# The scans of a hybrid block: VectorE's pieces in another order, squares and skip term in tiles of 64 columns

## What is computed

```python
x = x + conv_attention(group_norm(x))              # 1: softmax attention over 1024 pixels
t = to_tokens(x)                                   # 8 x 1024 tokens x 128
u = layer_norm(t)
xn = rmsnorm(u, norm_w)
z, xBC, dt = split(xn @ W_in.T)                    # 256 | 256+32+32 | 8
xBC = silu(causal_conv4(xBC) + conv_b)             # 4 taps along the tokens
xs, Bm, Cm = split(xBC)
dt = softplus(dt + dt_bias); dA = exp(-dt * exp(A_log))
state = state * dA + (dt * xs) B^T                 # a scan over the tokens, 8 heads of 32
y = state C + Dp * xs                              # Dp * xs is the skip term
y = rmsnorm(y * silu(z), gnorm_w)                  # needs the mean of (y * silu(z))^2
t = t + (u + y @ W_out.T)
t = t + mixture_of_8_experts(layer_norm(t))        # 3
```

## Time and profile before

| | us |
|---|---|
| three runs | 991.87, 996.23, 997.99 |
| median | 996.23 |
| profiled execution | 989.1 |
| its span, first to last instruction | 987.3 |
| busy in the span: TensorE / VectorE / ACT / GpSimd | 873.4 / 727.9 / 502.2 / 273.0 |
| granted TensorE clock, mean over the span | 0.95 |

### The profile page before, as it was taken

The page is one execution under the profiler, slowest core; times in us unless marked ns, Lnnn a source line. Parts: engine busy times, 40 slices in busy tenths (PEclk is TensorE's granted clock), DMA queues, the critical chain, the costliest instruction groups (busy, mean ns, idle before and its releaser), DMA issues.

```text
span 987.3 us, 18734 instructions
## 1 busy us (share of the span) xinstructions
PE 873.4 (88%) x7086; PEld 679.8 (69%) x7086; DVE 727.9 (74%) x1959; ACT 502.2 (51%) x740; POOL 273.0 (28%) x264
## 2 busy tenths in 40 slices
PE   3788999999989788898989797979789999999997
PEld 2556656655666666676767675757668888888887
DVE  2867678667867668576767777686868889888985
ACT  1525455545567564656565646464315544554453
POOL 0025111011000525242525252428513331233200
PEclk9979999999999789899979999989989999999999
DMA  5631011101101230303030303032000000000001
GB/s 146 187 136 22 1 22 22 22 1 22 23 1 30 45 75 1 74 2 74 2 74 2 74 1 75 2 74 66 2 1 1 22 23 22 2 22 22 23 1 43
DMA packets 30888, 36.07 MB, mean 37 GB/s; under 512 B 4560, under 2 KB 24912, under 8 KB 30800
## 3 DMA queue, kind: packets, MB, share of 16 engines
q1 hardware_dynamic: 29648, 30.68, 12.9%
q10 hardware_dynamic: 1152, 4.19, 1.2%
HBM read 21.50 MB, written 4.98 MB: 27 GB/s over the span
## 4 chain that ended last, share of the span: by engine, by line
PE 34%; DVE 18%; issue 4%; ACT 2%; POOL 2%; DVEq 0%; ACTq 0%; POOLq 0%
PE ps L1047 7%; DVE acc L1996 4%; PE ps L969 4%; PE ps L794 3%; PE ps L796 3%; PE ps L795 3%; DVE cacc L1712 2%; PE ps L960 2%; PE ps L948 2%; PE ps L953 1%; DVE dcy L1804 1%; PE ps L905 1%; PE ps L919 1%; PE ps L872 1%; PE ps L1088 1%
## 5 line engine op out<-in xcount | busy, mean ns | idle before, releaser
L1996 DVE SCALAR_TENSOR_TENSOR acc<-ps,comb,acc 128x128 f32<-128x128 f32 x512 | 139.8, 343 | 16.3 <-PE ps L1047 15.7
L1399 ACT ACTIVATE hid<-ps,b_f 128x512 f32<-128x512 f32 x128 | 87.2, 687 | 112.1 <-PE ps L796 112.0
L1047 PEld LDWEIGHTS ps<-w_f,hid 128*128 128x128 f32 x1024 | 130.6, 191 | 19.6 <-ACT hid L1399 8.1
L1047 PE MATMUL ps<-w_f,hid 128*128 128x128 f32 x1024 | 136.8, 277 | 5.2 <-ACT hid L1399 4.6
L1569 DVE TENSOR_REDUCE nmax<-ps 128x1 f32<-128x1024 f32 x64 | 78.1, 1220 | 29.8 <-PE ps L674 29.4
L1712 DVE SCALAR_TENSOR_TENSOR cacc<-ps,cw,cacc 128x1023 f32<-128x1023 f32 (+5 forms) x72 | 91.7, 1275 | 10.3 <-ACT cacc L1271 9.2
L570 POOL TENSOR_TENSOR srs<-sve,neg_half 128x1 f32<-128x1 f32 x64 | 53.8, 841 | 147.9 <-DVE gram L1821 147.8
L1187 ACT ACTIVATE probs<-ps,nmax 128x1024 f32<-128x1024 f32 x64 | 71.3, 1114 | 39.3 <-DVE nmax L1569 36.5
L969 PE MATMUL ps<-y_w 128*128 128x256 f32 x256 | 75.1, 420 | 12.8 <-DVE X L1831 12.2
L1340 ACT ACTIVATE dcy<-ps 128x1024 f32<-128x1024 f32 x64 | 65.1, 1017 | 40.8 <-PE ps L919 40.7
L1864 DVE TENSOR_TENSOR y_w<-ps,zs 128x256 f32<-128x256 f32 x64 | 27.0, 422 | 78.5 <-PE ps L960 76.0
(11 more groups left out here) (214 smaller groups left out, 1881.9 us busy)
## 6 DMA issues: line engine op xcount, KB each, us to landing
c_dec<-exp_dram SPq DMA_DIRECT2D x32, 256.0 KB, 5.1
xc<-in_x SPq DMA_DIRECT2D x8, 512.0 KB, 3.6
q_b<-q_a SPq DMA_DIRECT2D x16, 256.0 KB, 2.8
X<-in_x_tok ACTq DMA_DIRECT2D x8, 512.0 KB, 5.2
c_rep<-cacc SPq DMA_DIRECT2D x32, 128.0 KB, 5.9
out<-o_ch SPq DMA_DIRECT2D x8, 512.0 KB, 2.6
w_f<-in_w SPq DMA_DIRECT2D x2, 512.0 KB, 3.7
cst_f<-in_sel_rows SPq DMA_DIRECT2D x1, 512.0 KB, 4.3
```

The costliest lines, as they stand in the source:

```text
L1047: last = nc.tensor.matmul(ps[:, Y_BANKS[n], t * P:(t + 1) * P], hid[n % 2][:, t * P:(t + 1) * P], w2_f[:, e, :], start=True, stop=True)
L1399: nc.scalar.activation(hid[n % 2][:], ps[:, 4 + n % 2, :], ACT.Gelu, bias=b1_f[:, n // 2:n // 2 + 1]).then_inc(e_hidden_ready, 1)
L1996: done = nc.vector.scalar_tensor_tensor(acc[u][:, tt, :], ps[:, bank, t * P:(t + 1) * P], comb[u][:, tt, e:e + 1], acc[u][:, tt, :], ALU.m ...
```

## The change

Three things in the scans:

1. **Order.** `dve_parts` gets other slots: conv (0, 2) and (0, 3) join (0, 1) at slot 4 ahead of the gating; conv (1, 1) and (1, 2) go to slot 5; both halves of softplus to 5.5; conv (1, 3) to 6; `exponents` from 7.5 to 7, ahead of conv (2, 1); conv (2, 2) goes behind the end of the batch to -0.25 of the next and (2, 3) to its slot 0, behind `mixed` and `output`. TensorE's `cumulate` moves from slot 7.5 to 6.5. On ACT softplus moves from 5 to 4.5, `factors` from 7.5 to 7, and `shortcut` is divided into halves at slots 4 and 5.5 (before: whole at 6.5).
2. **Squares.** `out_product` makes the 128 output columns alone. Behind them come the squares in two column tiles: for each half of 64 tokens only the 64 x 64 block on the diagonal, in tiles of 128 x 64. `id_mean` and `gram` have 64 columns.
3. **Skip term.** The diagonal product is made of its two 64 x 64 blocks, in tiles at (0, 0) and (64, 64).

```diff
-        id_mean = sb("id_mean", [P, P])
+        id_mean = sb("id_mean", [P, 64])
...
                 for g in range(2):
-                    nc.tensor.matmul(o[:, g, :], d_diag[:, g, :], cacc[b % 3][:, g, t], start=(g == 0), stop=False,
-                                     skip_group_check=True)
+                    for j in range(2):
+                        r = slice(j * 64, (j + 1) * 64)
+                        nc.tensor.matmul(o[r, g, :], d_diag[r, g, r], cacc[b % 3][r, g, t], start=(g == 0), stop=False,
+                                         tile_position=(j * 64, j * 64), skip_group_check=True)
...
                 k = n % 4
                 for g in range(2):
-                    last = nc.tensor.matmul(ps[:, 6 + n % 2, DI:BANK].rearrange("p (k t) -> p k t", k=2), y_w[:, g, k, :],
-                                            y_w[:, g, k:5:4 - k, :], start=(g == 0), stop=(g == 1))
+                    nc.tensor.matmul(ps[:, 6 + n % 2, BANK - P:BANK], y_w[:, g, k, :], y_w[:, g, 4, :],
+                                     start=(g == 0), stop=(g == 1), skip_group_check=True)
+                for g in range(2):
+                    for j in range(2):
+                        r = slice(j * 64, (j + 1) * 64)
+                        last = nc.tensor.matmul(ps[r, 6 + n % 2, DI:DI + 64], y_w[:, g, k, r], y_w[:, g, k, r],
+                                                start=False, stop=(g == 1), tile_position=(0, j * 64),
+                                                skip_group_check=True)
...
-                        (group, (1, 1), 2, 4.5), (group, (2, 0), 2, 5.5), (group, (2, 1), 2, 5.5), (cumulate, (), 2, 7.5)]
+                        (group, (1, 1), 2, 4.5), (group, (2, 0), 2, 5.5), (group, (2, 1), 2, 5.5), (cumulate, (), 2, 6.5)]
...
-            def shortcut(b, u):
+            def shortcut(b, u, t0=0, t1=NT):
...
-                for t in range(NT):
+                for t in range(t0, t1):
...
-                last.then_inc(m_residual_ready, 1)
+                if t1 == NT:
+                    last.then_inc(m_residual_ready, 1)
...
-                         (tap, (1,), 2, 4.5), (softplus, (), 2, 5), (tap, (2,), 2, 5.5), (shortcut, (), 1, 6.5),
-                         (factors, (), 2, 7.5)]
+                         (shortcut, (0, 4), 1, 4), (tap, (1,), 2, 4.5), (softplus, (), 2, 4.5), (tap, (2,), 2, 5.5),
+                         (shortcut, (4, NT), 1, 5.5), (factors, (), 2, 7)]
...
-            dve_parts = [("conv", (2, 3), 1, -0.25), ("ends", (), 1, 1), ("low", (), 2, 2.75), ("inner", (), 1, 3),
-                         ("conv", (0, 1), 2, 4), ("steps", (), 2, 4.5), ("conv", (0, 2), 2, 4.5),
-                         ("conv", (0, 3), 2, 4.75), ("softplus", (0,), 2, 5.5), ("conv", (1, 1), 2, 5.5),
-                         ("conv", (1, 2), 2, 6), ("softplus", (1,), 2, 6.5), ("conv", (1, 3), 2, 6.5),
-                         ("conv", (2, 1), 2, 7), ("exponents", (), 2, 7.5), ("conv", (2, 2), 2, 7.5)]
+            dve_parts = [("conv", (2, 2), 1, -0.25), ("conv", (2, 3), 1, 0), ("ends", (), 1, 1), ("low", (), 2, 2.75),
+                         ("inner", (), 1, 3), ("conv", (0, 1), 2, 4), ("conv", (0, 2), 2, 4), ("conv", (0, 3), 2, 4),
+                         ("steps", (), 2, 4.5), ("conv", (1, 1), 2, 5), ("conv", (1, 2), 2, 5),
+                         ("softplus", (0,), 2, 5.5), ("softplus", (1,), 2, 5.5), ("conv", (1, 3), 2, 6),
+                         ("exponents", (), 2, 7), ("conv", (2, 1), 2, 7)]
...
-                nc.vector.scalar_tensor_tensor(gram[:], ps[:, 6 + n % 2, DI:DI + P], GN2_EPS * DI, id_mean[:], ALU.add,
+                nc.vector.scalar_tensor_tensor(gram[:], ps[:, 6 + n % 2, DI:DI + 64], GN2_EPS * DI, id_mean[:], ALU.add,
```

More of the change, by code:

```diff
@@ L185, in hybrid_kernel @@
         state = msb("state", [P, 2, DS, NT - 1])
-        gram = msb("gram", [P, P])
+        gram = msb("gram", [P, 64])
         sve = msb("sve", [P, 4])
@@ L1506, in scale_outputs @@
                     nc.vector.tensor_scalar(d_diag[:, g, :], id_f[:], d_col[:, g:g + 1], None, ALU.mult)
-                nc.vector.tensor_scalar(id_mean[:], id_f[:], 1.0 / DI, None, ALU.mult)
+                for j in range(2):
+                    r = slice(j * 64, (j + 1) * 64)
+                    nc.vector.tensor_scalar(id_mean[r], id_f[r, r], 1.0 / DI, None, ALU.mult)
             def high_weights():
```

## The result

The changed kernel took 958.06 us (median of four runs, 957.72 to 959.70) against 994.41 for the kernel before (four runs): a ratio of 0.965, with a 95% interval of 0.962 to 0.968. The profiled execution took 959.7 us, its span 957.9; before these were 989.1 and 987.3.

The account below looks back on a forecast made before the run. TensorE was taken as the bound, idle 32 us in batches 1 to 5, mostly behind VectorE's order. Steady batches 23.5, batch 0 6.3 and the last two 0.3 made 30: 989.1 to 959, 966 as median; range 955 to 979, widened to 954 to 988.

Parts of the forecast that it names:

- the walk: VectorE's new order in batch 2, timed instruction by instruction: a steady batch of 44.2 us at full clock.
- The walk's 2.0 us before the sums: TensorE's cumulative sums, moved ahead by a step, would newly wait 2.0 us for conv (1, 3).
- both large waits: TensorE's waits in batches 1 to 5 for expc (13.6 us) and X (8.9 us) would be all but gone.
- the signs in the last part: Checks named beforehand: waits, L1734, y_w(4) after three convolutions, batch of 45 to 46 us, 1.4 us to the 32x32 matmuls.
- its three terms: Uncertainties behind the forecast's own range: clock (10 us), softplus's first instruction L1734 (9), tiles (9).
- No difference: Tiles on TensorE: a step's output product, squares and skip term take 1.39 to 1.43 us, against 1.40 before.
- not on the path: VectorE's sum of squares reads 64 columns instead of 128: under 0.1 us, not counted.
- One stretch per batch: TensorE at half clock for 3.4 us in each steady batch, costing 1.7 us.
- The rival without such stretches (956): No half clock left, since no wait above 2.0 us is left: 1.7 us less in six batches, 956; chance 0.14.
- The clock did not take the gain: Rival: shorter matmuls bring two more half-clock stretches in each of eight batches, 27 us, giving 993; chance 0.10.
- The half-working order: Rival: softplus still meets GpSimd's product (+1.5 us), with a second half-clock stretch (+1.7): gain 11 us, 985; chance 0.18.
- slower: Rival: 64-column tiles do not run side by side; a step costs 2.47 us instead of 1.40, 1034 in all; chance 0.05.

Follow-up runs that it names:

- softplus_early: The new order with the old products, but the first half of softplus ahead of conv (1, 1): 978.4 us, ratio 0.984.
- conv0_late: The new order with the old products, but conv (0, 2) and (0, 3) back behind the small instructions of step 4: 993.0 us, ratio 0.998.

## Why the prediction was right, and where it was not

**The sum held for the steady batches; that all of it agrees is partly luck.** Against the profiled execution I forecast 959; it took 959.7. The steady batches gave 24.7 us for the 23.5 forecast. At full clock a batch takes 44.31 us (the shortest ones of the changed kernel's second profile) for the 44.2 of the walk, and 1.3 on top, most of it by the clock (45.6 in all), for the 1.7. The walk's 2.0 us before the sums is 1.9, and both large waits went, as written. The other terms missed by 1.6 to 1.8 us each and cancel: batch 0 gave less, the last two batches more, and the attention ahead of the scans took 1.6 us longer, with 46.1 us at half clock for 32.5. Of the signs in the last part five came: expc and X gone, the sums at 1.9 in each batch, L1745 at 0.19, y_w(4) 0.4 us behind the three convolutions (1.8 in the two batches with half clock there), a batch at 45.6. One did not: from the output product to the 32x32 matmuls it is 1.50 us, not 1.4.

**The offset failed.** I added 7.1 us, the distance of the median from the profiled execution. That took for granted that it would stay. After the change the profiled execution lies 1.6 us above its own median. The executions of the kernel before beside the last four runs spread over 987.6 to 996.0 us, with mean clocks of 0.95 for the five shortest and 0.93 to 0.94 for the rest; the changed kernel's over 956.2 to 960.6. So the profiled execution of before was one of the good ones, and the medians differ by 36 us, not by 29. What the others lose fits half clock behind waits that the change has removed, but no slower execution of before was traced, so that stays an argument. Nor does the prediction show how its three terms make the range of 955 to 979.

**Batch 0 and the last two.** I forecast 6.3 us for batch 0 and read 4.5. The wait of the sums is 1.6, for 2.2. What varies is the clock: in the changed kernel's second profile batch 0 took 57.2 us, with 21.7 at half clock against 11.9 in the first. The last batch gave 1.7, for 0.3 in both of the last two: again half clock (3.4 instead of 10.2 us in the two together).

**The tiles: right in sum, wrong in its terms.** "No difference" came out, but I had reckoned a step as equal, and it is 0.10 us longer on TensorE. The output product is 0.53 to 0.54 as forecast, the skip term 0.58 at my upper end; the squares take 0.38 where I had 0.32. The term that was too small is the change of shape. An eighth of the columns does take an eighth of the time: in the step shown above pairs of squares start 0.06 us apart (482.01, 482.07, 482.13). But the first pair, from 481.90, takes 0.11, and the first pair of the skip term 0.16 where the next takes 0.11. So a change costs the 0.10 us ahead of the new shape that I had, and 0.05 more on its first pair, twice in a step. What I had called "not on the path" makes up for it: the sum of squares on VectorE fell from 0.28 to 0.21 us, and VectorE sets the pace in part of the steps. In undisturbed batches the gap from y_w(0) to y_w(1) is 4.90 for 4.80 without the tiles, y_w(3) to y_w(4) 7.30 for 7.23, but y_w(5) to y_w(6) 5.40 for 5.47 and y_w(7) to the next 4.80 for 4.87. A batch is 44.3 either way. My rule "wrong if the pairs start 0.1 us apart" was not met: the tiles do run side by side.

**The clock.** One stretch per batch was forecast; there were four in five batches, and one in the second profile. Where they fall (changed kernel, 3.4 us before and after two falls):

```profile
467.60:471.00 3.40, 3.40 (x31) 3.21 (x30) 2.45 (x4) 2.59 (x4) 3.36 (x3) 1.00 0.02 5
471.00:474.40 3.40, 3.40 (x43) 2.29 (x45) 2.05 (x2) 1.71 (x6) 0.00 (x0) 0.51 0.00 0
573.50:576.90 3.40, 1.92 (x12) 1.61 (x12) 2.96 (x7) 0.50 (x2) 2.95 (x2) 0.99 0.00 0
576.90:580.30 3.40, 3.40 (x46) 2.31 (x48) 2.26 (x6) 1.21 (x3) 0.00 (x0) 0.50 0.08 19
```

The first came out of a stretch in which TensorE was busy throughout, with the small matmuls of `steps` in it, as in the earlier trace rows; the second behind the wait of the sums, with TensorE busy 1.92 us of 3.40. Two of the four are of each kind. Each makes its step 1.4 to 1.5 us longer (8.73 for 7.29; 6.05 for 4.59). The Trainium skill ("TensorE: Matmul & The Clock Gate", section "Why this matters for your kernels") lays drops to idle gaps; the second kind agrees, the first does not. The rival without such stretches (956) was nearer in its mechanism than its 0.14 says: the second profile has one.

**The other rivals.** The clock did not take the gain: 13.7 us at half in batches 1 to 5, for 37.5 before. With the tiles in the old order it rose to 51.2, in one profile each, but that kernel lost only 0.3%. The half-working order did not come, but `softplus_early` and `conv0_late` show that its conditions were the right ones: with softplus meeting the product (a wait of 4.2 us) the gain was 1.6%, with a wait of 4.5 us it was gone. I had set a longer wait's clock cost at one more 3.4 us stretch (1.7); in `conv0_late` the clock took 4.6 a batch. The first of the two I had priced well: 49.1 us a batch by the rival's 1.5 us of gain, 48.9 in `softplus_early`. But I had taken the two as one case, and in `conv0_late` nothing was left. The rival "slower" priced a square of 64 columns at 0.109 us, the time of 128; by the rate of the rows it would be half.

## What to carry to other kernels

A pause of one engine is the first place to look for room: 2.6 us of convolutions put into a 3.0 us pause made all the later moves worth something, and without it they were worth next to nothing. Walk the engine that feeds the bound instruction by instruction, and see how long its unbroken run is and which wait ends it; a wait of 2 us cost little beyond its own length, and with one of 4.5 us the clock took twice the wait's growth besides. Make a sum against the profiled execution, but before its distance from the median is added, ask whether that distance is made of the waits that the change removes.

## What the runs showed of the hardware

- **A product on GpSimd and a small instruction on VectorE.** In the changed kernel's batch 2 the product runs from 477.72 to 479.82, beside convolutions, which take one operand from PSUM and keep their length, and is over before softplus begins. GpSimd's timeline:

```profile
477.72 2.10 POOL L551 TENSOR_TENSOR c_dec<-c_dec,c_rep 128x896 f32<-128x896 f32 x1
...
486.38 1.46 POOL L570 TENSOR_TENSOR srs<-sve,neg_half 128x1 f32<-128x1 f32 x1 [0.25 <-DVE gram L1832]
```

  It works both ways: the root L570 takes 0.55 us in five of this batch's eight steps, and 1.46 to 1.47 in three, where VectorE's mixed (here 486.22, 1.22 long) started before it; `output` behind it then waits 0.44 us. In the kernel before it was two of eight; the walk had not foreseen the third. The Trainium skill ("SBUF — State Buffer", section "SBUF: two separate sides") describes such an exclusive lock; 0.19 against 1.76 us agrees.
- **Changes of tile shape.** The output product needs 0.53 us for matmuls of 0.43, so about 0.10 us stand before the first tile of the next shape; the first pair of that shape takes 0.05 us more than the later ones. The way back to the full shape, with the squares alone in tiles, costs 0.10 us before and 0.10 on the first matmul: the first two matmuls of the undivided skip term start 0.21 us apart (614.73 and 614.95), the next 0.11.
- **Half clock that costs nothing.** In the kernel before, the step from y_w(6) to y_w(7) took 5.34 to 5.35 us in all of batches 1 to 5, although 2.7 us of it were at half clock in batch 2 and 1.3 in batch 5. VectorE has no pause ahead of y_w(7) there and sets the pace. From y_w(3) to y_w(4), where VectorE waits for TensorE, 3.4 us at half clock turned 7.29 us into 8.74 to 8.83. Of the 37.5 us in these batches, 22.5 fell from y_w(7) on, where no batch was free of it, so their price can't be read.
